# A two-layer graph network: one gathered tile in 96 is fetched by 128 single-row transfers of SP

## The reference, cut to what matters

```python
# layer 0
h = relu(edge_feat @ W1 + b1);  w = (h @ W2 + b2).reshape(e, 4, 8, 8)
s_e, v_e = s[src], v[src]                       # the gather
m0 = ALPHA * (einsum('ei,eio->eo', s_e * sh0, w_000) + C110 * einsum('eim,em,eio->eo', v_e, sh1, w_110))
m1 = ALPHA * (einsum('ei,em,eio->eom', s_e, sh1, w_011) + einsum('eim,eio->eom', v_e * sh0, w_101))
x = _layernorm(x + segment_sum(messages, dst) + self_part)
# layer 1
R = relu(abs_distances @ w1 + b1) @ w2 + b2
Fj = features[src]                              # the gather, from the rows that layer 0 made
msg = ...                                       # Rb, Fb, spherical harmonics of rel_vec, per edge
x = _layernorm(x + out.at[dst].add(msg))
```

## Time and profile before

| | |
|---|---|
| median of 3 runs | 4162.87 us |
| profiled execution, its own time | 4169.84 us |
| its span | 4168.0 us |
| granted TensorE clock, mean | 0.90 |
| GpSimd (POOL) busy | 3004.4 us, 72% |
| VectorE busy | 3469.6 us, 83% |
| TensorE matmul busy | 3391.4 us, 81% |
| gathers | 3136, half in each layer |

### The profile page before, as it was taken

How to read it: one execution, slowest core, us unless ns; L and a number is a source line. 1 busy time by engine, 2 the same in 40 slices (tenths; PEclk the granted TensorE clock), 3 DMA queues, 4 the chain that set the end, 5 groups by cost and what they waited for, 6 DMA issues and landing times.

```text
span 4168.0 us, 76267 instructions
## 1 busy us (share of the span) xinstructions
PE 3391.4 (81%) x23178; PEld 1952.9 (47%) x23178; DVE 3469.6 (83%) x5246; ACT 2181.1 (52%) x6573; POOL 3004.4 (72%) x3143
## 2 busy tenths in 40 slices
PE   5777777777777777777459999999999999999995
PEld 3444444444444444444235555555555555555553
DVE  8888788888878888887759988888888888888887
ACT  3555555555555555555336655555555555555553
POOL 5777777777777777777277777777777777777772
PEclk7888888888888888888779999999999999999998
DMA  3111111111111111111212212122121212121212
GB/s 104 33 30 33 29 35 33 29 33 29 33 29 35 33 29 33 29 33 29 34 35 44 47 37 47 37 47 46 38 48 37 47 37 47 37 47 37 47 37 31
DMA packets 220966, 159.83 MB, mean 38 GB/s; under 512 B 125489, under 2 KB 194994, under 8 KB 220466
## 3 DMA queue, kind: packets, MB, share of 16 engines
q0 software_dynamic: 100352, 51.58, 8.6%
q1 hardware_dynamic: 84946, 90.16, 8.4%
q10 hardware_dynamic: 35650, 17.88, 1.6%
HBM read 148.94 MB, written 10.43 MB: 38 GB/s over the span
## 4 chain that ended last, share of the span: by engine, by line
POOL 42%; issue 25%; DVE 15%; PE 7%; DMA 7%; DVEq 2%; POOLq 0%; SPq 0%; ACT 0%; ACTq 0%
POOL rows L364 42%; PE red L687 4%; DVE prod L977 3%; DMA src<-in_src 3%; PE wps L674 2%; DMA rows<-in_x,src 2%; DMA rows<-x_rows,src 2%; DVE prod L983 1%; DVE q L1032 1%; DVEq L1060 1%; DVE q L1042 1%; DVE prod L970 1%; PE wps L667 1%; DVE table L1056 1%; DVE rest L998 0%
## 5 line engine op out<-in xcount | busy, mean ns | idle before, releaser
L364 POOL DMA_INDIRECT rows<-x_rows,src x1568 | 1509.8, 963 | 569.4 <-issue 564.9
L364 POOL DMA_INDIRECT rows<-in_x,src x1568 | 1493.8, 953 | 508.5 <-issue 494.6
L687 PE MATMUL red<-prod,ident 128*128 128x336 f32 (+1 forms) x4704 | 1492.2, 471 | 0.0
L687 PEld LDWEIGHTS red<-prod,ident 128*128 128x128 f32 x4704 | 883.0, 193 | 626.5 <-issue 180.9
L667 PE MATMUL wps<-bias_parts,ones 64*128 64x448 bf16 (+1 forms) x2352 | 479.8, 405 | 694.3 <-DVE prod L977 490.8
L983 DVE TENSOR_TENSOR prod<-wps,q 128x896 f32<-128x896 f32 x784 | 835.1, 1082 | 185.3 <-PE wps L674 168.2
L493 ACT ACTIVATE gap<-iota,slot_plan 128x128 bf16<-128x128 f32 x3136 | 935.6, 386 | 7.0
L674 PE MATMUL wps<-w_sb,hidden 64*128 64x448 f32 (+1 forms) x3920 | 753.6, 480 | 0.0
L511 ACT ACTIVATE sums<-red 128x336 f32<-128x336 f32 (+1 forms) x294 | 136.3, 464 | 1082.3 <-PE red L687 1081.7
L667 PEld LDWEIGHTS wps<-bias_parts,ones 64*128 64x128 bf16 x2352 | 115.3, 95 | 1230.7 <-DVE prod L977 607.2
L674 PE MATMUL wps<-w_oi,hidden 64*128 64x256 f32 (+1 forms) x2352 | 533.5, 579 | 0.0
(11 more groups left out here) (126 smaller groups left out, 3205.6 us busy)
## 6 DMA issues: line engine op xcount, KB each, us to landing
mlp<-in_dist SPq DMA_DIRECT2D x196, 256.0 KB
mlp<-in_feat SPq DMA_DIRECT2D x98, 256.0 KB
rows<-in_x,src POOLq DMA_INDIRECT x1568
rows<-x_rows,src POOLq DMA_INDIRECT x1568
frames<-frame ACTq DMA_DIRECT2D x49, 144.0 KB, 1.8
geo<-frames ACTq DMA_DIRECT2D x98, 72.0 KB
src<-in_src SPq DMA_DIRECT2D x196, 8.0 KB
geo<-in_sh ACTq DMA_DIRECT2D x98, 32.0 KB, 1.7
```

Source lines behind the costliest of these rows:

```text
L364: nc.gpsimd.indirect_dma_start(out=rows[z][:, t, :], out_offset=None, in_=table_rows, in_offset=bass.IndirectOffsetOnAxis(ap=src_sb[z][:, ...
L687: ins = nc.tensor.matmul(red[:, bank * 512:bank * 512 + cols], ident[:], pr[:, i, :, a:b, :], start=(i == 0), stop=(i == MUL - 1))
```

## The change

One tile in 96 is no longer gathered by GpSimd: the last tile (t = 15) of every sixth chunk, 16 tiles in each layer. Its 128 source indices come in an input of their own (`src_fetched`). SP loads them, reads them four at a time into registers, and issues for each edge a DMA of one row of 128 bytes into the buffer `fetched`. These 128 DMAs are spread over the six chunks of a block as 24, 24, 20, 20, 20 and 20. When all have landed, one DMA moves `fetched` into `rows[1][:, 15, :]`. VectorE and ScalarE wait for it (`tile_moved`) besides the gathers. GpSimd issues 95 gathers in a block and adds the missing 16 to `rows_gathered[1]` with one INC_SWDGE_SEM. The loops run over 16 blocks of three rounds, and the 49th round is written out behind them. SP's order changes too: for each chunk it now loads `src` and directly after it `mlp`.

```diff
+FETCH_PARTS = (24, 24, 20, 20, 20, 20)
+FETCH_CHUNKS = len(FETCH_PARTS)
+FETCH_ROUNDS = FETCH_CHUNKS // RING
+FETCHES = ROUNDS // FETCH_ROUNDS
...
+            def fetch_rows(n, part):
+
+                table_rows = x if n == 0 else x1
+                p0 = sum(FETCH_PARTS[:part])
+                for p in range(p0, p0 + FETCH_PARTS[part], 4):
+                    _, indices = nc.values_load_multi_w_load_instructions(
+                        fetch_index[0:1, p:p + 4], engines=(mybir.EngineType.SP,), min_val=0, max_val=N_NODES - 1,
+                        skip_runtime_bounds_check_because="the indices of the edges' sources are rows of the table")
+                    for a, index in enumerate(indices):
+                        sp.dma_start(fetched[p + a:p + a + 1, :], table_rows[bass.ds(index, 1), :]
+                                     ).then_inc(row_fetched, 16)
...
+                    with sp.Fori(0, FETCHES) as h:
+                        f = sp.snap(j * FETCHES + h + 1 + n * (count * FETCHES))
+                        r0 = round_of(sp, j, h * FETCH_ROUNDS)
+                        sp.dma_start(fetch_index[:], src_fetched[bass.ds(h, 1), :]).then_inc(indices_loaded, 16)
+                        for m in range(FETCH_CHUNKS):
+                            z = m % RING
+                            r = round_of(sp, j, h * FETCH_ROUNDS + m // RING)
+                            k = h * FETCH_CHUNKS + m
+                            load_source(n, z, r, k)
+                            load_mlp(n, z, r, k)
+                            if m == 0:
+                                sp.wait_ge(s.tile_moved, r0 * 16)
+                                sp.sem_inc(s.tile_moved, (FETCH_ROUNDS - 1) * 16)
+                                sp.wait_ge(indices_loaded, f * 16)
+                                if n == 1:
+                                    sp.wait_ge(x1_stored, 16)
+                                sp.sem_inc(fetch_turns, 1)
+                            fetch_rows(n, m)
+                        sp.wait_ge(row_fetched, 16 * P)
+                        sp.sem_clear(row_fetched)
+                        sp.wait_ge(s.rows_read[RING - 1], r)
+                        sp.wait_ge(s.rows_copied[RING - 1], r)
+                        sp.dma_start(rows[RING - 1][:, TILES - 1, :], fetched[:]).then_inc(s.tile_moved, 16)
...
-                for t in range(TILES):
+                for t in range(tiles):
                     nc.gpsimd.indirect_dma_start(
                         out=rows[z][:, t, :], out_offset=None, in_=table_rows,
                         in_offset=bass.IndirectOffsetOnAxis(ap=src_sb[z][:, t:t + 1], axis=0),
                     ).then_inc(s.rows_gathered[z], 16)
+                if tiles < TILES:
+                    pool.inc_swdge_sem([s.rows_gathered[z]], [(TILES - tiles) * 16], mode="add")
...
-                    with pool.Fori(0, ROUNDS) as i:
-                        r = round_of(pool, j, i)
-                        for z in range(RING):
-                            gather(n, z, r)
+                    with pool.Fori(0, FETCHES) as h:
+                        for m in range(FETCH_CHUNKS):
+                            gather(n, m % RING, round_of(pool, j, h * FETCH_ROUNDS + m // RING),
+                                   TILES - (1 if m == FETCH_CHUNKS - 1 else 0))
+                    for z in range(RING):
+                        gather(n, z, round_of(pool, j, ROUNDS - 1))
```

More of the change, by code:

```diff
@@ L139, in build @@
         span = sb("span", [P, 4])
+        fetch_index = sb("fetch_index", [1, P], I32)
+        fetched = sb("fetched", [P, FEAT])
         span_max = sb("span_max", [P, 2])
@@ L305, in _, with load_source, load_mlp @@
                     sp.sem_inc(semaphore, count)
+                sp.sem_inc(s.tile_moved, 16)
             sp.sem_inc(frames_stored, 16)
             sp.dma_start(rel_sb[:], rel).then_inc(loaded["rel"], 16)
+            def load_source(n, z, r, k):
+                s = layers[n]
+                sp.wait_ge(s.rows_read[z], r)
+                sp.dma_start(src_sb[z][:], src[bass.ds(k, 1)].rearrange("k p t -> p (k t)")
+                             ).then_inc(s.src_loaded[z], 16)
+            def load_mlp(n, z, r, k):
+                s = layers[n]
+                if n == 0:
+                    sp.wait_ge(s.hidden_summed[z], r * 2)
+                    sp.dma_start(mlp_sb[z][:, 0:SET], feat[bass.ds(k, 1)].rearrange("k p c -> p (k c)")
+                                 ).then_inc(s.mlp_loaded[z], 16)
+                else:
+                    sp.wait_ge(s.hidden_ready[z], r * 2)
+                    for a in range(2):
+                        sp.dma_start(mlp_sb[z][a * HID:(a + 1) * HID, :],
+                                     dist[bass.ds(k, 1), a, :].broadcast_to([HID, CHUNK // 2])
+                                     ).then_inc(s.mlp_loaded[z], 16)
+            def fetch_rows(n, part):
[8 more added lines that the diff above has]
+                                     ).then_inc(row_fetched, 16)
             def stream(n, count):
```

38 lines of the change are left out of this document (18 added, 20 removed).

## The result

| | before | after |
|---|---|---|
| median of 5 runs each, us | 4166.0 (4162.75 to 4167.18) | 4096.9 (4093.47 to 4097.7) |
| profiled execution, its own time, us | 4169.84 | 4094.89 |
| granted TensorE clock, mean | 0.90 | 0.905 |

The ratio is 0.9834, 95% interval 0.9821 to 0.9848. The change saves 69 us by the medians and 75 by the two profiled executions. The forecast was 33, and its range ended at 4118: the sign was right, and the size was wrong by a factor of two. Three of the later kernels (e14, e15 and e16) ran on a chip where the kernel before took 6886.04 us at a granted clock of 0.75, so their times are compared with that alone.

A forecast was written before the change was run, and what follows sets the result against it. GpSimd's stream of gathers was taken to set the pace of both layers. Profiled execution: 4169.84 - 40.9 + 7.4 + 0.9 = 4137.2 us; on the median 4162.87 - 32.6 = 4130 us; range 4118 to 4162 us.

The forecast's parts named there:

- GpSimd's stream sets the pace of both layers: On GpSimd: its stream of gathers bounds both layers, 1992 + 2013 of 4168 us.
- layer 1 does not follow: Rival on layer 1: something besides gathers is late, only layer 0's half remains; 4147 us, or 4150; chance 0.11.
- 16 gathers a layer, 40.9 us: On GpSimd: 16 gathers fewer per layer at the average pitch, 1.271 and 1.285 us each, save 20.3 + 20.6 us.
- INC_SWDGE_SEM, +7.4 us, bounds from nothing up: On GpSimd: 32 instructions added behind blocks of 95 gathers, 0.23 us each; bounds from no cost to 80 us.
- dry queue: Rival on GpSimd: its queue runs dry at every INC_SWDGE_SEM, costing 27 us; 4150 us; chance 0.22.
- long pause paid: Rival at each block's end on GpSimd: INC_SWDGE_SEM also pays the long pause, 80 us in all; 4203 us; chance 0.07.
- The pitch holds the long pauses too, which come by the number of gathers.: On GpSimd: the average pitch pricing the removed gathers, 1.271 and 1.285 us, was taken to include the long pauses.
- SP, 0.57 us per row: On SP: each fetched row costs 0.57 us, 128 rows 73 us; a block costs 82 and 87 us.
- SP as the limit: Rival on SP: row issues outlast GpSimd's block, deciding from 0.87 us per row; +419 us, 4582 us; chance 0.10.
- The rule against the change: On SP's small transfers: about 2.0 us fixed per DMA, if serial 256 us per block and far over 8 ms.
- The starts: At each layer's start: the index row's DMA goes ahead of the first `src`, 0.44 us twice, 0.9 us.

The follow-up runs named there:

- e14: The kernel before, with GpSimd itself waiting ahead of each chunk for its own gathers' count; on the 6886.04 us chip, 6854.75 us, ratio 0.9954.
- e15: The kernel after with two tiles instead of one missing from GpSimd's gathers in each sixth chunk; on the 6886.04 us chip, 7033.2 us, ratio 1.0213.
- e16: The kernel after, with GpSimd itself waiting ahead of each chunk for its own gathers' count; on the 6886.04 us chip, 6989.58 us, ratio 1.0153.
- e15b: e15 again at normal speed: the kernel after with 94 gathers per block, one missing tile keeping old rows; 4046.63 us, ratio 0.9718.
- e4_no_inc: The kernel after without INC_SWDGE_SEM in the block, the 95th gather adding 32 instead of 16 to the count; 4096.89 us, ratio 0.984.
- e18b_one_missing_once: The kernel before with one gather left out a single time per layer, in its third chunk, its semaphore raised by 16 instead; 4161.36 us, ratio 0.9991.
- e7_rows_twice: The kernel after with each row fetched twice by SP, the second time into a buffer nobody reads; 4444.9 us, ratio 1.0671 to before.
- e17_other_count: e10_spare_gather, but SP waits for the spare gather and tells GpSimd by another semaphore; 4123.12 us, ratio 0.9902 to before.
- e12_after_add_each: The kernel after with an INC_SWDGE_SEM behind every chunk, adding 16 to the gathers' own count, 32 where the tile is missing; 4094.87 us, ratio 0.9833.
- e5_fetch_only: The kernel after with all 96 gathers on GpSimd and no INC_SWDGE_SEM, SP's fetches going to a buffer nobody reads; 4167.49 us, ratio 1.0008.
- e10_spare_gather: The kernel after plus one spare gather per block into an unread buffer, on its own semaphore, for which GpSimd itself waits; 4124.86 us, ratio 0.9903.

## Why the prediction was wrong in size

- *GpSimd's stream sets the pace of both layers*: right. Layer 0 and layer 1 gained 37.6 and 38.4 us; "layer 1 does not follow" did not happen.
- *16 gathers a layer, 40.9 us*: right as far as it goes. e15b takes 16 more out of each layer, and gains 50 us more by the medians: 40 for the gathers, and most of the rest for the pauses, whose time above 0.30 fell from 13 us to 5, all of it waits for indices in layer 1.
- *INC_SWDGE_SEM, +7.4 us, bounds from nothing up*: mis-sized. It took 0.39 to 1.96 us each and cost nothing that can be measured (e4_no_inc): the first ran from 137.70 to 139.34 on the sequencer while gathers started at 137.98 and 139.23 with their usual 0.30 us. The lead of 12 gathers that the prediction read in the earlier trace rows hides it. The two rivals built on it, dry queue and long pause paid, fall with it.
- *The step that failed* is the sentence "The pitch holds the long pauses too, which come by the number of gathers." I counted 16 gathers at an average pitch, and so gave the change 1% of the pauses. Their number does go by gathers (13 to 11 that are seen), but their length goes by where the 113th gather falls against the end of a chunk, and this the change moves, by a single gather. It was worth 16 us in layer 0 and 20 in layer 1 (some 2 of these from waits for indices), half of the gain. e18b_one_missing_once shows the step by itself: 0.80 us where the place has moved, 1.85 to 2.09 where it has not. The numbers were in the rows: 1.95 and 1.91 us, 142 us apart, which is 7 chunks of 16. A pause whose period is a whole number of chunks had a phase to be asked about, and it should have widened the range downward: 21 + 27 us could vanish, which gives 4082. Two errors had the same sign: the forecast without the INC_SWDGE_SEM is 4123, still 26 us above the result.
- *SP, 0.57 us per row*: 0.57 measured (2.26 us for four rows), partly by luck, for the parts were off in both directions (the issue 0.23 instead of 0.445 with its register work, the load of four 0.56 instead of 0.5, the arithmetic 0.04, the rest gaps). A block cost 119.7 - 34 = 86 us in layer 0 and 121.0 - 28 = 93 in layer 1, against 82 and 87 foreseen. SP as the limit: not at 0.57, but at two issues per row (e7_rows_twice, 4444.9 us).
- *The rule against the change*: a fixed cost of every small transfer, paid in series, would have shown as 8 ms; the waits for the last rows of a block were 15.6 + 15.9 us in all 32 blocks, 1 us each, so latencies overlap. By this the rule of the Trainium skill on small transfers ("DMA: Bandwidth & Descriptors", "Rules for kernel authors") does not price these: they cost their issue. The 2.0 us that the prediction quotes stand in a section on GpSimd's transfers, and these are SP's.
- *Layer 1 does not follow*: the prediction's second figure for this rival, 4150, is 4151 by its own terms; it changes nothing.
- *The starts*: 1.3 us later at the first gather; 0.9 were charged for both layers.

## What to carry to other kernels

When a stream that sets the pace has a second, rarer pause, find its period in units of the program (gathers, chunks) before pricing a change by an average pitch: if the period is a whole multiple of a block, any change of the block's size moves the phase, and with it the pause can change: here from 1.95 us to 0.7, and with one more gather out to nothing. Test it with the smallest disturbance, one instruction left out once, and see to it that the disturbance moves the pause against the blocks: one gather more at the start moved both and told nothing. And an operation that looks dear in its own record can be free if its sequencer runs ahead of the engine; ask how many instructions the lead is.

## What the runs showed of the hardware

- GpSimd's indirect DMAs of 128 rows go out one per 1.25 us (0.944 and 0.305), but behind 113 of them the next is held up. The price was 1.95, 0.7 or 0 us with one, two or three gathers between the last complete chunk and the stop, where the sequencer had its lead, and 2.25, 1.45 or 0.65 where it had none (e14, e16 and e7, e15 and e7). The Trainium skill ("SBUF — State Buffer", "SBUF size: 192, 224, or 256?") says that a part of each partition is kept back for the descriptors of GpSimd's DMAs. That this is the record which fills at 113 was not tried.
- One spare gather in each 96, on a semaphore of its own, removed the stops, and made a kernel with all 96 gathers a block 41 us faster than before (e17_other_count, 4123.12 us). A kernel that has both the 95 gathers and no stops should come to some 4084 to 4087 (an estimate: 4096.9 less 5.3 and 7.6, of which about 3 are waits for indices that e17 has too), for instance with one of the needed gathers on a semaphore of its own; it was not tried. Of the kernels with the whole output none is faster than after: e12_after_add_each's 4094.87 is not distinguishable from it.
- SP issues a transfer of one row, with its address from a register, in 0.228 us, and 4096 of them beside 3136 gathers cost at most 0.17% (e5_fetch_only: 1.0008, 0.9998 to 1.0017).
- INC_SWDGE_SEM takes longer the more gathers were issued since the last stop: 0.39 to 1.96 us in after; 1.65 to 1.66 in every block of e10_spare_gather. It runs on the sequencer, with some 12 gathers still to start (at 137.70 us 83 of the 95 ahead of it had started), and costs nothing that can be measured.
